# Similarity's left side and the first graph product without norms: where the norms go in, and where the swap stands in SyncE's queue

## The reference, cut to what matters

```python
xf = x.reshape(B, C, N).transpose(0, 2, 1)
nrm = jnp.linalg.norm(xf, axis=-1, keepdims=True)
xn = xf / jnp.maximum(nrm, 1e-12)
sim = jnp.einsum('bnc,bmc->bnm', xn, xn)
val, idx = jax.lax.top_k(sim, K)                 # K = 9
v = val / (val.sum(axis=-1, keepdims=True) + 1e-06)
def gcn_apply(feat, w, b):
    xt = feat @ w
    neigh = jax.vmap(lambda t, i: t[i])(xt, idx)
    return jnp.einsum('bnkc,bnk->bnc', neigh, v) + b
out = gcn_apply(xn, w1, b1)      # then group norm and silu
out = gcn_apply(of, w2, b2)      # then group norm, silu, and + x1
```

## Time and profile before

| what | value |
|---|---|
| median of 3 runs | 685.54 us (684.87 to 685.59) |
| the profiled execution | 687.54 us |
| its span in the profile | 685.7 us |
| busy: PE, PEld, DVE, ACT, POOL | 621.9, 310.4, 536.6, 449.2, 499.2 us |
| granted TensorE clock, mean | 0.98 |

### The profile page before, as it was taken

One profiled execution on the slowest core, in us unless ns is written; L12 is line 12 of the kernel. 1 busy time (PEld: TensorE's weight loads), 2 busy tenths in 40 slices (PEclk: granted clock), 3 DMA queues, 4 the chain that ended last, 5 costly groups with the idle time before them and its releaser, 6 DMA issues.

```text
span 685.7 us, 12336 instructions
## 1 busy us (share of the span) xinstructions
PE 621.9 (91%) x3824; PEld 310.4 (45%) x3824; DVE 536.6 (78%) x1008; ACT 449.2 (66%) x942; POOL 499.2 (73%) x534
## 2 busy tenths in 40 slices
PE   8878899898999999898999999999999999899874
PEld 6654535353444535353544435353535444333441
DVE  3357879788898889797888988898898988857821
ACT  2356477685868767784868768786868686743321
POOL 0224877788797978879797978788897979786810
PEclk9999999999999999999999999999999999979997
DMA  3002533434353535444363634445353534353411
GB/s 94 1 17 46 115 72 79 88 83 96 81 110 69 109 77 110 80 90 92 80 109 62 113 79 108 87 87 100 91 94 63 109 77 98 74 108 78 63 32 31
DMA packets 148722, 55.76 MB, mean 81 GB/s; under 512 B 138008, under 2 KB 138512, under 8 KB 148656
## 3 DMA queue, kind: packets, MB, share of 16 engines
q1 hardware_dynamic: 148656, 54.97, 39.6%
HBM read 12.87 MB, written 4.32 MB: 25 GB/s over the span
## 4 chain that ended last, share of the span: by engine, by line
PE 33%; POOL 24%; issue 16%; DVE 10%; DMA 9%; ACT 7%; SPq 1%; POOLq 0%; ACTq 0%; DVEq 0%
PE pC L974 18%; POOL adj L389 10%; PE pS L930 5%; POOL adj L384 5%; DMA rbc<-rn_row 4%; DMA rn_row<-rnT 4%; ACT adj L527 2%; PE pB L775 2%; DVE kstat L607 2%; ACT ek L458 2%; POOL res L407 2%; PE pA L814 2%; POOL qn L348 2%; POOL xn L372 2%; DVE top L683 2%
## 5 line engine op out<-in xcount | busy, mean ns | idle before, releaser
L974 PE MATMUL pC<-adj,xt 128*64 128x512 f32 x992 | 233.1, 603 | 2.9 <-POOL adj L395 1.6
L389 POOL TENSOR_TENSOR adj<-maskT,adj 128x128 f32<-128x128 f16 (+3 forms) x127 | 163.5, 1287 | 27.0 <-DMA maskT<-mask 25.2
L683 DVE MAX8 top<-pS 128x8 f32<-128x1024 f32 x128 | 155.6, 1224 | 33.1 <-ACT adj L527 32.9
L701 DVE MATCH_REPLACE8 mask<-top,pS 128x1024 uint16<-128x1024 f32 x128 | 155.2, 1213 | 0.0
L930 PE MATMUL pS<-xn 64*128 64x512 f32 x256 | 146.9, 661 | 7.3 <-issue 6.5
L930 PE MATMUL pS<-xn,xsw 64*128 64x512 f32 x256 | 146.2, 662 | 2.9 <-DVE mask L701 2.9
L527 ACT COPY adj<-pS 128x1024 f32<-128x1024 f32 x128 | 128.3, 1003 | 30.3 <-PE pS L932 30.2
L384 POOL TENSOR_TENSOR adj<-maskT,adj 128x128 f32<-128x128 f16 (+6 forms) x111 | 128.4, 1157 | 0.0
L974 PEld LDWEIGHTS pC<-adj,xt 128*64 128x64 f32 x992 | 64.0, 137 | 103.3 <-issue 94.7
L395 POOL TENSOR_TENSOR adj<-adj,selves 128x128 f32<-128x128 f32 x127 | 58.5, 461 | 8.7
L932 PEld LDWEIGHTS pS<-mark,place 64*128 64x128 f16 x256 | 24.7, 97 | 77.3 <-issue 77.3
(11 more groups left out here) (154 smaller groups left out, 1097.0 us busy)
## 6 DMA issues: line engine op xcount, KB each, us to landing
xs<-x SPq DMA_DIRECT2D x32, 128.0 KB, 2.8
vbc<-v_row SPq DMA_DIRECT2D x32, 128.0 KB, 2.9
rbc<-rn_row SPq DMA_DIRECT2D x30, 128.0 KB, 2.9
xsw<-xn SPq DMA_DIRECT2D x30, 128.0 KB, 2.3
out<-res SPq DMA_DIRECT2D x30, 128.0 KB, 2.3
maskT<-mask SPq DMA_TRANSPOSE x128, 3.1
cst<-packed SPq DMA_DIRECT2D x1, 471.5 KB, 3.6
y1sw<-y SPq DMA_DIRECT2D x2, 128.0 KB, 2.3
```

The lines of the kernel that those rows point to most:

```text
L389: pool.tensor_tensor(above, m[:, r, 0:r + 1, :].bitcast(F16), above, ALU.mult).then_inc(done["upper"], 1)
L683: dve.max(top[b % 2][:, r, 0:TOP], pS[r % 2][:, :]).then_inc(done["tile_top"], 1)
L701: dve.match_replace(out=mask[n % MASKS][:, :], in_to_replace=top[b % 2][:, r, 0:TOP], in_values=pS[r % 2][:, :], imm_value=ONE_BITS).then_ ...
L974: mm = pe.matmul(ps[h * C:(h + 1) * C, 0:H], xt[:, t % NJ, t // NJ, :], adj[b % 2][:, t, h * H:(h + 1) * H], start=(t == 0), stop=(t == NT ...
```

## The change

`y1`, `xsw` and `rn` change their parts:

- Similarity's left side is `y1` (now two buffers) instead of `xn`. `xsw` holds the exchanged halves of `y1`. A row of a tile then lacks the factor `rn` of its own token. It is put in when ACT takes the tile out of PSUM: the copy becomes an activation with a scale per partition. The largest eight of a row and their places are the same; DVE multiplies the eight values of all tiles by `rn` once per sample, ahead of `vtot`.
- The first graph product takes `y1` as well, so TensorE's L945 waits for `y1` and no longer for `xn`. DVE, not ACT, takes it out of PSUM and multiplies by `rn` on the way (stage `tokens`).
- `rn` gets two buffers; its step on POOL waits for two older steps more. POOL's `xn` no longer waits for an older swap.
- On SP the swap waits for `y1` instead of `xn`, and its place in `TIMES` changes from 139.8554 to 111.8545.
- Sample 0 had a way of its own, with eight more matmuls and a second multiply on DVE for its `xsw`. It now takes the general way.
- Scales in powers of two keep the mask's mark below all similarities.

```diff
-XSCALE = 0.25
+XSCALE = 2.0 ** -12
-MARK = -2.5 * SSCALE
+MARK = -2.5 / 16
...
     "sync": {
-        "unit": [122.814, 124.0739, 139.8554],
+        "unit": [111.8545, 122.814, 124.0739],
...
     "vector": {
+        "tokens": [121.5],
...
@@ SP
             def unit(b):
+                yield
+                sp.wait_ge(*of("y1_ready", b))
+                sp.wait_ge(*of("sim_ps", b - 2, NT))
+                for h in range(2):
+                    sp.dma_start(xsw[b % 2][(1 - h) * C:(2 - h) * C, :], y1[b % 2][h * C:(h + 1) * C, :]).then_inc(done[f"swapped{b % 2}"], 16)
                 if b == 0:
...
-                yield
-                sp.wait_ge(*of("xn_ready", b))
-                sp.wait_ge(*of("sim_ps", b - 2, NT))
-                for h in range(2):
-                    sp.dma_start(xsw[b % 2][(1 - h) * C:(2 - h) * C, :], xn[b % 2][h * C:(h + 1) * C, :]).then_inc(done[f"swapped{b % 2}"], 16)
@@ POOL
-                if b > 2:
-                    pool.wait_ge(*swapped(b - 2))
-                pool.tensor_tensor(xn[b % 2][:, :], y1[:, :], rbc[:, :], ALU.mult).then_inc(done["xn_ready"], 1)
+                pool.tensor_tensor(xn[b % 2][:, :], y1[b % 2][:, :], rbc[:, :], ALU.mult).then_inc(done["xn_ready"], 1)
@@ ACT
-                yield
-                act.wait_ge(*of("xt1_ps", b))
-                act.wait_ge(*of("g1_ps", b - 2))
-                act.copy(xt1[b % 2][:, :, :, :], pB[:, :].rearrange("p (j h c) -> p j h c", j=NJ, h=2)).then_inc(done["xt1_copied"], 1)
...
+                    act.wait_ge(*of("rn_ready", b))
-                    act.copy(adj[b % 2][:, r, :], pS[r % 2][:, :]).then_inc(done["sim_copied"], 1)
+                    act.activation(adj[b % 2][:, r, :], pS[r % 2][:, :], ACT.Copy, scale=rn[b % 2][:, r:r + 1]).then_inc(done["sim_copied"], 1)
@@ DVE
+            def tokens(b):
+
+                yield
+                dve.wait_ge(*of("xt1_ps", b))
+                dve.wait_ge(*of("g1_ps", b - 2))
+                norms = rn[b % 2][:, :].rearrange("p (h j) -> p j h", h=2).unsqueeze(3).broadcast_to([P, NJ, 2, C])
+                dve.tensor_tensor(xt1[b % 2][:, :, :, :], pB[:, :].rearrange("p (j h c) -> p j h c", j=NJ, h=2), norms,
+                                  ALU.mult).then_inc(done["xt1_copied"], 1)
...
+                best = top[b % 2][:, :, 0:TOP]
+                dve.tensor_tensor(best, best, rn[b % 2][:, :].unsqueeze(2).broadcast_to([P, NT, TOP]), ALU.mult).then_inc(done["top_scaled"], 1)
@@ TensorE
-                    src = xn if r // NJ == h else xsw
+                    src = y1 if r // NJ == h else xsw
...
-                pe.wait_ge(*of("xn_ready", b))
+                pe.wait_ge(*of("y1_ready", b))
```

More of the change, by code:

```diff
@@ L157, in build @@
         x1 = [sb(f"x1_{i}", [P, H]) for i in range(XBUFS)]
-        y1 = sb("y1", [P, H])
+        y1 = [sb(f"y1_{i}", [P, H]) for i in range(2)]
         sq = sb("sq", [P, H])
         xn = [sb(f"xn{i}", [P, H]) for i in range(2)]
-        y1sw = sb("y1sw", [P, H])
         xsw = [sb(f"xsw{i}", [P, H]) for i in range(2)]
         ssq = sb("ssq", [P, NT])
-        rn = sb("rn", [P, NT])
+        rn = [sb(f"rn{i}", [P, NT]) for i in range(2)]
         rnT = sb("rnT", [NT, P])
@@ L361, in unit @@
                 pool.wait_ge(*of("ss_read", b, 2))
-                pool.tensor_tensor(rn[:, :], ssq[:, :], minus_half[:, :], ALU.pow).then_inc(done["rn_ready"], 1)
+                pool.wait_ge(*of("sim_copied", b - 2, NT))
+                pool.wait_ge(*of("v_tot", b - 2))
+                pool.tensor_tensor(rn[b % 2][:, :], ssq[:, :], minus_half[:, :], ALU.pow).then_inc(done["rn_ready"], 1)
                 yield
@@ L501, in unit @@
                 act.wait_ge(*of("mi_bias", b))
-                act.wait_ge(*of("xn_ready", b - 1))
-                act.activation(y1[:, :], x1[b % XBUFS][:, :], ACT.Identity, bias=st["mi"][:, 15:16],
+                act.wait_ge(*of("sim_ps", b - 2, NT))
+                act.activation(y1[b % 2][:, :], x1[b % XBUFS][:, :], ACT.Identity, bias=st["mi"][:, 15:16],
                                scale=st["mi"][:, 13:14]).then_inc(done["y1_ready"], 1)
@@ L506, in unit @@
                 act.wait_ge(*of("y1_ready", b))
-                act.activation(sq[:, :], y1[:, :], ACT.Square).then_inc(done["sq_ready"], 1)
+                act.activation(sq[:, :], y1[b % 2][:, :], ACT.Square).then_inc(done["sq_ready"], 1)
             def itself(b):
@@ L667, in unit @@
                     dve.wait_ge(done["rows"], 1)
-                    dve.tensor_tensor(xn[0][:, :], pB[:, :], y1[:, :], ALU.mult).then_inc(done["xn_ready"], 1)
-                    dve.wait_ge(done["rows"], 2)
-                    dve.wait_ge(done["exchanged"], 32)
-                    dve.tensor_tensor(xsw[0][:, :], pC[:, :], y1sw[:, :], ALU.mult).then_inc(done["first_swapped"], 1)
+                    dve.tensor_tensor(xn[0][:, :], pB[:, :], y1[0][:, :], ALU.mult).then_inc(done["xn_ready"], 1)
                 else:
@@ L907, in unit @@
                 if b == 0:
-                    for bank, other in ((pB, 0), (pC, 1)):
-                        for j in range(NJ):
-                            for h in range(2):
-                                t = (h ^ other) * NJ + j
-                                mm = pe.matmul(bank[h * C:(h + 1) * C, j * P:(j + 1) * P], rn[:, t:t + 1].broadcast_to([P, C]), ident,
-                                               start=True, stop=True)
-                        mm.then_inc(done["rows"], 1)
+                    for j in range(NJ):
+                        for h in range(2):
+                            t = h * NJ + j
+                            mm = pe.matmul(pB[h * C:(h + 1) * C, j * P:(j + 1) * P], rn[0][:, t:t + 1].broadcast_to([P, C]), ident,
+                                           start=True, stop=True)
+                    mm.then_inc(done["rows"], 1)
                 else:
-                    pe.transpose(pB[0:NT, P:2 * P], rn[:, :], ident).then_inc(done["rn_T"], 1)
+                    pe.transpose(pB[0:NT, P:2 * P], rn[b % 2][:, :], ident).then_inc(done["rn_T"], 1)
             def similarity(b, r):
@@ L922, in similarity @@
                     pe.wait_ge(*of("xn_ready", b))
-                    pe.wait_ge(*swapped(b))
+                    pe.wait_ge(*of_buffer("swapped", b, 2, 32))
                 warm(f"sim{r}", b)
@@ L944, in neighbours @@
                 for j in range(NJ):
-                    mm = pe.matmul(pB[:, j * P:(j + 1) * P], xn[b % 2][:, j * P:(j + 1) * P], w1[:, :], start=True, stop=True)
+                    mm = pe.matmul(pB[:, j * P:(j + 1) * P], y1[b % 2][:, j * P:(j + 1) * P], w1[:, :], start=True, stop=True)
                 mm.then_inc(done["xt1_ps"], 1)
```

17 lines of the change are left out of this document (7 added, 10 removed).

## The result

| what | before | after |
|---|---|---|
| median of 4 runs each, in one set | 685.57 us (684.87 to 689.58) | 841.97 us (837.75 to 846.81) |
| the profiled execution | 687.54 us | 837.75 us |
| its span | 685.7 us | 836.0 us |
| granted TensorE clock, mean | 0.98 | 0.89 |

The changed kernel is slower: 1.227 times the time of before (95% interval 1.219 to 1.235). The forecast was 832 us, with a range of 805 to 868.

A forecast was written before the change was run, and what follows sets the result against it. No engine alone but a loop through several was taken as the bound, 37.3 us a round. On the profiled 687.5 us, 121.8 + 21 + 1.5 + 4 - 1 - 1 = +146.3 gave 833.8, as median 832 us, range 805 to 868.

The forecast's parts named there:

- The swap holds SP, and `vbc` with it: SP stops for `y1` ahead of T2, `v_row` and `vbc`; `kstat` is 8.7 us late in 14 rounds, 121.8 us.
- the start's: Swap of sample 1 stands ahead of T2 of sample 0, which comes late: 4 us, between 0 and 5.2.
- the sign to look for: In the new trace SP should wait for ACT's `y1`, some 14 times 8 us.
- The rule of dispatch: DMA engines do not wait on semaphores; the issuing sequencer waits before it dispatches, so SP stops at the swap.
- The rival on the other side: SP not held, the swap leaves the path: 674 us, faster; chance 0.05, of which 0.04 faster and 0.01 within.
- The low clock: TensorE resumes at half clock after a pause of about 8 us: 1.5 us a round, 14 rounds, 21 us.
- The scaled copy: ACT's 128 copies of 1.003 us become scaled activations, +0.11 each; one per round in the loop, 1.5 us in all.
- DVE's two new instructions: Product with `rn` from PSUM, 0.68 us, and scaling of 64 values, 0.23, behind the last mask: cost nothing.
- The cover of 0.78 us: Behind the last mask DVE idles 0.78 us for ACT's first tile, which hides 0.78 of 0.91 us of new work.
- own bound without cover, 15 us: If DVE's idle time hid none of its new work, it would cost 0.9 x 16 = 15 us.
- the large term: SP's stop at the swap, delaying `vbc` and `kstat`: 14 x 8.7 = 121.8 us.
- the small ones: TensorE's clock +21, ACT's copy +1.5, start +4, less swap waiting -1, sample 0 -1, DVE's new work nothing.

The follow-up runs named there:

- The wait alone: Kernel before plus one wait: SyncE waits for `y1` of the next sample ahead of each sample's T2, issuing nothing more there; 810.2 us, ratio 1.176.
- the pause filled: Changed kernel with 76 matmuls of zeros per sample in TensorE's pause ahead of step `ss`, samples 2 to 14; 836.8 us, ratio 1.219 (with 60: 854.7 us).
- the product alone: Kernel before plus one DVE product of 64 elements per sample ahead of `vtot`, result unused; 688.6 us, ratio 1.0012.
- the arithmetic alone: Changed kernel with the swap of `y1` at the old swap's place, 699.4 us, or between the `rn_row` store and `rbc` load, 695.2 us.

## Why the prediction came out as it did

- **The swap holds SP, and `vbc` with it: right.** 8.7 us a round were forecast; `y1` to `kstat` grew by 112.7 us over the 13 rounds in which it shows, 8.67 each. With 6.9 us behind the last `y1`, where the 14th hold lies, and 5.8 in the first round, where the start's lies, that is 125.4 us, against 121.8 + 4. The wait alone gives 122 us with its clock loss. Only the sign to look for was misread: SP's waits are 11 us, not 8, though the reads are late by the 8.9 that were forecast.
- **The rule of dispatch: right.** The wait is SP's own, and what was issued behind it came behind it. The rival on the other side needed `y1` 8.7 us earlier; it came as ever.
- **The low clock: right in kind, somewhat large in size.** 1.5 us a round were taken. `kstat` to `rnT` grew by 15.4 us in 13 rounds, 1.18 each, of which 0.10 is the copy (5.84 against 5.74 us without the hold), so 1.1 for the clock in this step. Part of the last step's growth may be clock as well: two of its rounds, of 29.7 and 27.9 us, have 6.8 and 3.4 us at half clock in it. With the pause filled this step lost 11.6 us of its length, and the rounds without half clock in it are back at 5.83.
- **The scaled copy: right.** 1.106 us against the 1.113 of the earlier trace rows.
- **DVE's two new instructions, priced at nothing: the step that failed.** "The scaling of 64 values is near the reduction of 80, 0.23": it took 1.31 in the median of after. The row chosen had its size, but one input. The trace of before had a row with two inputs in SBUF beside POOL, 1.87 us for 128 elements (L725), and it was overlooked. The cover of 0.78 us was real (the product alone cost nothing in the kernel before), yet product plus `xt` came to 2 us. The prediction's own bound without cover, 15 us, is near what the last step grew by (19.6). Of this, 6.2 come with the wait alone (358.6 us in that run) and 6.4 with the arithmetic alone; the rest is there only with both. The size of the instruction is shown. That it, and not the clock and the waits of the stretched round, made the step 19.6 us longer is shown for no part of them.
- **A gain that was not foreseen** covers half of that: `rnT` to `xn` is 0.65 us a round shorter. The wait alone shows it too (75.3 against 84.4 us), so it comes with the stretched round and not with the arithmetic. That its DMAs meet less other traffic is only argued.
- **The sum**, 832 against 842 measured, came close because the large term held, and by luck in the small ones: 20 us missing in one step met 9 of unforeseen gain and some 7 too much for the clock. In the profiled executions it is 834 against 838. Without the hold the small terms decide the sign: the arithmetic alone was expected level or faster, and is 7 to 11 us slower. No version here beats the kernel before.

## What to carry to other kernels

On a queue that issues in order, ask of a step that is moved forward not whether its data is used early, but when its own wait ends and who stands behind it; one wait that ended 8 us late cost 18% with all arithmetic unchanged. Price a small VectorE instruction by its inputs as well as its size: with two tensors in SBUF, or from SBUF to SBUF with a scalar, it ends only behind a GpSimd instruction that has begun before it, and each instruction pays anew. Here the one with an input in PSUM was the cheaper form, and eight small ones were the worst. What a held instruction costs depends on who waits behind it: one product cost nothing in the kernel before, and a move of the scaling to another place made two kernels 11 and 17 us slower. Look for such an instruction in the trace that you have before you price it from one of its size.

## What the runs showed of the hardware

- The held 64-element products end 0.07 to 0.09 us after the end of POOL's instruction beside them, in seven kernels. POOL's durations stay nearly as they were (L381 1288 ns in the mean of after, 1278 with eight held instructions a sample). But POOL is held in the same way when a longer instruction of DVE has begun first: 2.88 us instead of 1.9 for 128x896 in before.
- With 3.2 us of a pause left open, the granted clock fell to 0.52 in the dense work that followed, for 6.1 us; with 8.4 us open it was 0.51 for the first 3.5 us of work. A step of 5.83 us at full clock took 6.4 to 7.2 us with such stretches.
- Eight `tensor_scalar` instructions of eight or seven columns, some 0.2 us each at their shortest, took 9.6 and 10.3 us in a row beside a busy GpSimd. Those of one column kept their 0.27 us.
